# Weights kept in float32 and converted by the DMA: the ring of weight loads moves from SyncE to GpSimd

## What is computed

```python
x  = inputs                                  # 2 x 4096 x 4096
h  = layernorm(x)
h  = conv1d(h, conv_w, width=3) + conv_b     # 4096 -> 3072, split in q, k, v
q, k, v = h[..., :1024], h[..., 1024:2048], h[..., 2048:]
qh, kh, vh = q @ wq + bq, k @ wk + bk, v @ wv + bv      # 16 heads of 64
p  = softmax(causal(qh @ kh.T / 8))          # in blocks of 128 rows
o  = (p @ vh) @ wo + bo
x  = x + layernorm(o @ proj_w + proj_b)      # 1024 -> 4096
y  = layernorm(x)
gate = y @ gate_w.T + (y @ gate_a.T) @ gate_b.T         # 4096 -> 11008
up   = y @ up_w.T   + (y @ up_a.T)   @ up_b.T
hid  = silu(gate) * up
d  = hid @ down_w.T + (hid @ down_a.T) @ down_b.T       # 11008 -> 4096
x  = x + layernorm(d)
```

## Time and profile before

| | |
|---|---|
| time, median of 2 runs | 6074.04 us (5856.76 and 6291.31) |
| the profiled execution | 5857.6 us, its span on core 7 5854.9 us |
| TensorE matmuls | busy 5123.7 us (88% of the span), 24388 instructions |
| VectorE, ScalarE, GpSimd | busy 716.7, 445.4 and 5.3 us |
| queue of the ring (SP, hardware) | 739.16 MB, 44.1% of 16 DMA engines |
| queue of GpSimd (software) | 12.58 MB, 0.6% |
| read from device memory, written | 764.83 MB, 16.78 MB |

### The profile page before, as it was taken

How to read it: one execution, slowest core, us unless ns; L and a number is a source line. 1 busy time by engine, 2 the same in 40 slices (tenths; PEclk the granted TensorE clock), 3 DMA queues, 4 the chain that set the end, 5 groups by cost and what they waited for, 6 DMA issues and landing times.

```text
span 5854.9 us, 60933 instructions; the slowest of 8 cores (5847.8 to 5854.9 us)
## 1 busy us (share of the span) xinstructions
PE 5123.7 (88%) x24388; PEld 2359.0 (40%) x24388; DVE 716.7 (12%) x943; ACT 445.4 (8%) x801; POOL 5.3 (0%) x15
## 2 busy tenths in 40 slices
PE   1999763999999999999739996659999999999995
PEld 1444331444444444444324443324444444444442
DVE  3000326000000000000150004250000000000003
ACT  1000122000000000000020002210000000000001
POOL 0000000000000000000000000000000000000000
PEclk7999886999999999999969997979999999999998
DMA  3555320555555554555545552215555555545554
GB/s 111 152 151 151 97 65 19 153 152 153 153 152 153 152 154 124 143 143 143 157 148 151 151 151 63 73 46 153 152 153 153 153 152 152 152 123 142 143 143 132
DMA packets 402606, 785.66 MB, mean 134 GB/s; under 512 B 44832, under 2 KB 53024, under 8 KB 399264
## 3 DMA queue, kind: packets, MB, share of 16 engines
q1 hardware_dynamic: 399168, 739.16, 44.1%
q10 hardware_dynamic: 2304, 30.04, 1.3%
q0 software_dynamic: 864, 12.58, 0.6%
HBM read 764.83 MB, written 16.78 MB: 133 GB/s over the span
## 4 chain that ended last, share of the span: by engine, by line
PE 87%; DVE 7%; ACT 3%; issue 1%; DMA 1%; DVEq 0%; ACTq 0%; SPq 0%
PE pA L75 31%; PE pB L75 31%; PE pC L75 11%; PE pD L75 11%; DVE ssum L75 3%; PE pO L75 2%; DVE r L75 2%; PE pT L75 2%; ACT p_bf L75 1%; DVE stage_tm L75 1%; ACT stage_pf L75 1%; ACT stage_dn L75 1%; DMA r<-xs 1%; DVE p_bf L75 0%; DMA halo<-xs 0%
## 5 line engine op out<-in xcount | busy, mean ns | idle before, releaser
L75 PE MATMUL pA<-xln,ring 128*128 128x512 bf16 x5056 | 1116.3, 380 | 22.4 <-DMA ring<-conv_s 22.4
L75 PE MATMUL pB<-xln,ring 128*128 128x512 bf16 x5056 | 1113.0, 379 | 0.0
L75 PEld LDWEIGHTS pA<-xln,ring 128*128 128x128 bf16 x5056 | 494.1, 98 | 626.3 <-issue 27.3
L75 PEld LDWEIGHTS pB<-xln,ring 128*128 128x128 bf16 x5056 | 493.7, 98 | 601.4
L75 PE MATMUL pC<-xln,ring 128*128 128x512 bf16 x2752 | 608.0, 379 | 0.0
L75 PE MATMUL pD<-xln,ring 128*128 128x512 bf16 x2752 | 608.0, 379 | 0.0
L75 PE MATMUL pB<-hidden,ring 128*128 128x512 bf16 x2752 | 599.2, 379 | 0.0
L75 PE MATMUL pA<-hidden,ring 128*128 128x512 bf16 x2752 | 599.2, 379 | 0.0
L75 PE MATMUL pT<-id_b,stage_tm 128*128 128x128 bf16 x640 | 73.2, 306 | 398.3 <-DVE stage_tm L75 396.9
L75 PEld LDWEIGHTS pD<-xln,ring 128*128 128x128 bf16 x2752 | 269.3, 98 | 324.7
L75 PEld LDWEIGHTS pC<-xln,ring 128*128 128x128 bf16 x2752 | 269.2, 98 | 324.7
(11 more groups left out here) (108 smaller groups left out, 1702.1 us busy)
## 6 DMA issues: line engine op xcount, KB each, us to landing
ring<-gu_s SPq DMA_DIRECT2D x1032, 256.0 KB, 2.6
ring<-dn_s SPq DMA_DIRECT2D x640, 256.0 KB, 2.7
ring<-conv_s SPq DMA_DIRECT2D x576, 256.0 KB, 2.6
ring<-gu_s SPq DMA_DIRECT2D x344, 288.0 KB, 2.8
ring<-pj_s SPq DMA_DIRECT2D x64, 256.0 KB, 2.6
out<-r ACTq DMA_DIRECT2D x8, 2048.0 KB, 6.7
ring<-dn_s SPq DMA_DIRECT2D x64, 224.0 KB, 2.5
r<-xs ACTq DMA_DIRECT2D x4, 2048.0 KB, 8.2
```

Source lines behind the costliest of these rows:

```text
L75: r = getattr(eng, meth)(*args, **kwargs)
```

## The change

All weight tensors and the constants `lcon` are declared in device memory as float32, and the conversion to bf16 outside of the kernel is dropped. The buffers on chip stay bf16, so each load of weights now reads 4 bytes and writes 2 for each element, and converts on the way. These loads (ring, `wv_hold`, `lora`) move to GpSimd's queue. In exchange the `xs` loads of the second half move from GpSimd to SyncE, with the waits that they had. `lora` counts on semaphore y in place of x. In the diff one declaration stands for eight (`qk_s`, `wv_s`, `wo_s`, `pj_s`, `gu_s`, `dn_s` and `lcon` change likewise), and one dropped `.astype(BF)` for all eight arrays. The number, order and size in elements of all loads, the ring and all arithmetic stay.

```diff
@@ WStream._issue @@
-            "sy", "dma_start",
+            "gp", "dma_start",
             self.buf[:, s * RING_COLS: s * RING_COLS + cols], src,
             waits=(("te", self.freeval[s]),), inc=W_SEMS[s],
@@ build_nc @@
-    conv_s = nc.dram_tensor("conv_s", [CC3, 128, 96 * 128], BF16, kind="ExternalInput").ap()
+    conv_s = nc.dram_tensor("conv_s", [CC3, 128, 96 * 128], F32, kind="ExternalInput").ap()
...
-    p.op("sc", "dma_start", lora[:, :], lcon, inc="x")
-    v_lcon = p.cnt["x"]
+    p.op("gp", "dma_start", lora[:, :], lcon, inc="y")
+    v_lcon = p.cnt["y"]
...
-            p.op("sy", "dma_start", wv_hold[:, 0:4096], wv_s[:, 0:4096],
+            p.op("gp", "dma_start", wv_hold[:, 0:4096], wv_s[:, 0:4096],
                  waits=(("ve", v_halo_done),), inc="y")
-            p.op("sy", "dma_start", wv_hold[:, 4096:8192], wv_s[:, 4096:8192], inc="y")
+            p.op("gp", "dma_start", wv_hold[:, 4096:8192], wv_s[:, 4096:8192], inc="y")
...
-                         waits=(("ve", v_xln2), ("x", v_lcon)) + (bwait(pbn) if kc == 0 else ()),
+                         waits=(("ve", v_xln2), ("y", v_lcon)) + (bwait(pbn) if kc == 0 else ()),
...
-                        nxt_xv[0] = ("p0", p.op("gp", "dma_start", halo[:, 0:D],
+                        nxt_xv[0] = ("p0", p.op("sy", "dma_start", halo[:, 0:D],
...
-                        nxt_xv[5] = ("p5", p.op("gp", "dma_start", halo[:, D:2 * D],
+                        nxt_xv[5] = ("p5", p.op("sy", "dma_start", halo[:, D:2 * D],
...
-                    nxt_xv[g + 1] = (ps_, p.op("gp", "dma_start", r[:, g * D:(g + 1) * D],
+                    nxt_xv[g + 1] = (ps_, p.op("sy", "dma_start", r[:, g * D:(g + 1) * D],
@@ _prep @@
-    ).astype(BF)
+    )
```

More of the change, by code:

```diff
@@ L123, in build_nc @@
     xs = nc.dram_tensor("xs", [1280, D], F32, kind="ExternalInput").ap()
-    conv_s = nc.dram_tensor("conv_s", [CC3, 128, 96 * 128], BF16, kind="ExternalInput").ap()
[L125 to L131, removed]
+    conv_s = nc.dram_tensor("conv_s", [CC3, 128, 96 * 128], F32, kind="ExternalInput").ap()
+    qk_s = nc.dram_tensor("qk_s", [2, 8, 128, 1024], F32, kind="ExternalInput").ap()
+    wv_s = nc.dram_tensor("wv_s", [128, 8192], F32, kind="ExternalInput").ap()
+    wo_s = nc.dram_tensor("wo_s", [8, 128, 1024], F32, kind="ExternalInput").ap()
+    pj_s = nc.dram_tensor("pj_s", [DC, 128, 1024], F32, kind="ExternalInput").ap()
+    gu_s = nc.dram_tensor("gu_s", [MCH, 2, 128, 33 * 128], F32, kind="ExternalInput").ap()
+    dn_s = nc.dram_tensor("dn_s", [DC, 128, 87 * 128], F32, kind="ExternalInput").ap()
+    lcon = nc.dram_tensor("lcon", [128, 2400], F32, kind="ExternalInput").ap()
     biasb_in = nc.dram_tensor("biasb", [128, 122], F32, kind="ExternalInput").ap()
@@ L829, in _prep @@
     qk_s = np.ascontiguousarray(
-        np.stack([qk_lay(a("L0_attn_wq")), qk_lay(a("L0_attn_wk"))])).astype(BF)
+        np.stack([qk_lay(a("L0_attn_wq")), qk_lay(a("L0_attn_wk"))]))
     wv_s = np.ascontiguousarray(
         a("L0_attn_wv").reshape(8, 128, 1024).transpose(1, 0, 2).reshape(128, 8192)
-    ).astype(BF)
+    )
     wo_s = np.ascontiguousarray(
         a("L0_attn_wo").reshape(8, 128, 8, 128).transpose(2, 1, 0, 3).reshape(8, 128, 1024)
-    ).astype(BF)
+    )
     pj_s = np.ascontiguousarray(
         a("L0_attn_proj_w").reshape(8, 128, 32, 128).transpose(2, 1, 0, 3).reshape(32, 128, 1024)
-    ).astype(BF)
+    )
     def gu_lay(w, b, row0):
@@ L850, in _prep @@
         gu_lay(a("L0_ffn_up_w"), a("L0_ffn_up_b"), 32),
-    ], axis=1)).astype(BF)
+    ], axis=1))
     dwpad = np.zeros((32, 128, 128), f32)
@@ L865, in _prep @@
         aT_lay(a("L0_ffn_gate_a"), 32), aT_lay(a("L0_ffn_up_a"), 32),
-        aT_lay(a("L0_ffn_down_a"), 86)], axis=1)).astype(BF)
+        aT_lay(a("L0_ffn_down_a"), 86)], axis=1))
     biasb = np.zeros((128, 122), f32)
```

## The result

| | before | after |
|---|---|---|
| median, us | 5858.69 (12 runs) | 5880.27 (14 runs) |
| ratio to before, undisturbed executions | | 1.0037, 95% interval 1.0026 to 1.0048 |
| span of the profiled execution, us | 5854.9 | 5877.2 |
| read from device memory, MB | 764.83 | 1504.42 |

The change costs 22 us, 0.4%. That is less than the 2% that I took for what can be told, though the interval excludes zero. The forecast was 6270, and the outcome is near rival A (5870), to which I had given 0.39.

What follows compares the result with a forecast made beforehand. TensorE bounds the kernel now; converted loads at 240 ns a tile would take over. From 5858 us: stream +104, +275, +56, query and key +5, ring lead -46, starts +20, lcon +1, giving about 6270; range 5850 to 7300.

Steps and rivals of the forecast that it cites:

- rival A: Streaming stages: converted loads stay hidden behind TensorE's matmuls, only the two starts and lcon cost; 5870 us, chance 0.39.
- p = 240: Ring loads: a converted row (4096 B in, 2048 B out) costs one DMA engine 240 ns, hidden only below TensorE's 216.
- All three stream terms: Slower weight tiles in convolution +104, gate and up +275, down +56 us, less 46 for ring slots filled ahead.
- query and key: Query and key stage: its 2 x 128 weight tiles slow from 219 ns each, +5 us.
- The line through two rows of the trace: Price of plain loads: line through rows of 2112 B and 16384 B puts a 4096 B row at 200 ns.
- The factor of 1.18 for the software queue: Ring loads: software queue costs 1.18 times the hardware queue, raising a row from 200 to 236 ns.
- Bytes in plus bytes out: Ring loads: the converting engine pays for bytes in and out one after the other, 6144 B, 246 ns.
- The backlog of the earlier trace: wv and first ring loads queued together moved about 400 GB/s a core, so a plain 4096 B row takes 164 ns.
- The sign of the DMA share: Gate and up: share of 0.9 or more would show the forecast right, 0.75 to 0.95 would show rival A.
- The starts: Convolution start in each half: first matmul waits behind wv's doubled bytes on POOL, +10 us each, +20 in all.
- lcon: Kernel's beginning: lcon, doubled to 1.2 MB and moved to POOL, shares the DMA engines with the first xs load, +1 us.
- rival C: Streaming stages: POOL's issuing of loads becomes the bound above 1.74 us a load; 6290 us at 1.94, chance 0.12.

Runs made afterwards that it cites:

- e2: The kernel after the change with 7 matmuls left in every ring slot of the convolution, gate and up, and down stages, loads unchanged: 5460.36 us.
- e3: The kernel after the change with 3 of 8 matmuls left in each ring slot of the three streaming stages, loads unchanged: 5400.8 us.
- e1: A separate kernel of loads alone, eight stretches of 72 varying queue, source and type: from device memory 207 ns a converted row, 207 and 201 plain f32.
- e4: The kernel after the change with all weights in bf16 in memory again, queues as after the change, nothing converted: 5857.6 and 5858.02 us.
- e10: The kernel after the change with five ring slots instead of six: 5921.78 us.
- e8: The kernel after the change with four ring slots instead of six: 6564.41 us.

## Why the prediction was wrong

**The step that failed is the price of a converted row.** I set p = 240 ns, above TensorE's 216, by taking the software queue as 1.18 times dearer and the converting engine as paying for bytes in plus bytes out; e2 and e3 measure 198, below it, and neither surcharge exists in e1. All three stream terms (+104, +275, +56, less 46) hang on it and are zero, and query and key with them.

- *The line through two rows of the trace* gave 200 ns for a plain row of 4096 B. The number was right, 198 in the stream and 201 to 207 in e1, but partly by luck: it was a line of busy time, and the busy time of the converted row in the kernel after is 0.993 x 800 / 449 / 8.25 = 214 ns a tile on core 3, at a pace of TensorE's 216.
- *The factor of 1.18 for the software queue* was wrong. It came from the earlier trace rows, where one queue only loaded `xs` and the other only stored to `out`, and where both ran at once; I had the other comparison, 1.03, beside it, and took the larger. e1 has 207 on the hardware queue and 201 on the software queue, e4 no difference in time. Without the factor the first way gives 200 and the forecast would have been rival A.
- *Bytes in plus bytes out* gave 246 as a second way, and its closeness to 236 made me sure. They were two wrong numbers that agreed. On-chip, where nothing else limits, conversion adds at most 6% to a plain row, not 50% (e1).
- *The backlog of the earlier trace rows*, 400 GB/s and 164 ns, overrated what there is: I read 13 us on one core, and of those the later part, and rival A's "on all cores at once" was wrong. Its nine slices from 3031.9 to 3034.85 have 277 GB/s in the mean; core 6 beside it moved about 400 GB/s until some 3035 us and little after, and from then on core 7 had 366 to 429. That is what e1 shows too: 332 GB/s with the neighbour loading, 418 without. Over hundreds of us the cores get 331 GB/s. The change passed with 9% to spare (216 to 198), not the 32% that 164 ns would leave.
- *The sign of the DMA share* couldn't decide: I gave 0.9 or more to the forecast and 0.75 to 0.95 to rival A, and rival A came with 0.96. All the other signs of rival A held, and so did my sign that the forecast is wrong if a converted row costs as little as a plain one.

The Trainium skill (HBM Reference, Specifications) has 358 GB/s for each of two cores that stream, by which I estimated 183 ns a tile. The trace gives 331 and 198: the estimate was on the right side of TensorE's 216 ns, the page's rate 8% more than this kernel's loads got.

**The starts**: right in cause and nearly in size, the size partly by luck. I wrote +20 for the two at p = 240; they are +16.8. With the measured 198 ns the same working gives 64 x 0.198 - 5.2 = 7.5 us each, 15 in all. Rival A's +10 for them was too low, since the backlog behind them moves at 331, not 400 GB/s. **lcon**: +1 expected, +2.3 measured; e4, with lcon in bf16 on the same queue, doesn't have it (VectorE's first block at 56.59 to 57.69 us on its four later cores, 58.73 to 61.04 after the change). **xs on SP**: nothing expected, and VectorE's wait for it appears in the first half alone, as before. **POOL**: the 0.53 us of the earlier trace rows held for converting loads, 528 ns; rival C is out. **The clock**: the stream kept 1.00, as I had said. In e3, with TensorE busy 461.83 of 800 us in gate and up on core 0, the granted clock was 0.89 there, between its two levels (1.2 and 2.4 GHz), so at that shortage of weights it did fall. **Landing time**: I did not look at it. It doubled from 2.6 to 5.4 us, and only because the ring has six slots did that cost nothing in the stream: with five the change would have cost 1.1%, with four 12% (e10, e8).

## What to carry to other kernels

Work out a load's room from the rate that it needs and a saturated rate, not from the busy share: at a share of 0.97 there were 9% left. Measure that rate with both cores of a pair loading: a core alone got 418 GB/s here, and 332 beside a loading neighbour. A load that converts f32 to bf16 cost here what its reads cost, so it was all but free, as reading twice the bytes stayed under that saturated rate and the ring was deep enough for the longer landing time. Look for what stands behind a waiting load on its queue: issuing the ring loads ahead of it, with wv in pieces, gave 0.4% to the kernel before.

## What the runs showed of the hardware

- The cores' saturated rate for 4096 B rows from device memory was 331 GB/s each with all 8 loading (e3), for 2048 B rows 576 x 16 x 2048 B in 69.55 us, 271 GB/s (e1, ends included); from on-chip memory 4096 B rows took 165 ns an engine, 397 GB/s.
- The two cores of a pair share that rate: core 0 went from 332 to 418 GB/s when core 1 stopped loading from device memory (e1), core 4 from 315 to 423 after core 5 did.
- A load that converts cost the same as a plain f32 load from device memory (207 ns a row both), and at most 6% more from on-chip memory (e1).
- The DMA share rose to 1.07 under saturation (e2, e3), so 1 is no ceiling.
- A bf16 load of 128 rows of 2048 B took 80 packets on the software queue and 144 on the hardware queue (e4), in the same time.
- Between the release of a slot and its refilled use lie 6.2 us for a converted f32 load of 256 KB written, of which 5.2 are the landing, at a DMA share of 0.87 (e8).
